# Turning x with VectorE instead of identity products on TensorE, for groups two to four of a two-layer transformer kernel

## The chip, the cores and the metric

The kernel runs on one core of one Trainium2 chip. The metric is device time in microseconds (us) for one execution. PE is TensorE, DVE is VectorE, ACT is ScalarE, POOL is GpSimd and SP is SyncE, which issues most of the DMAs. The times of the kernel before are 1934.53, 1934.77 and 1935.47 us.

## What is computed

The input x holds 32 batches of 64 tokens with 1024 features, in fp32. Two layers follow, each with a residual. What the change touches is the front of the first layer:

```python
# layer 0: a per-batch 64x64 matrix over the 64 tokens (the mixing), then a 1024x1024 weight
W = L0_cond_weights[itok_B_0_15]
mixed = einsum('bct,bcd->bdt', x, W)
x1 = x + mixed @ effective_weight.T + b_base      # effective_weight = W_base + adapters through a Fourier table
# layer 1: gate/up/down with per-batch adapters, then a product with sign(weight)
act = silu(x1 @ W_gate.T + lora) * (x1 @ W_up.T + lora)
x2 = x1 + (act @ W_down.T + lora) @ sign(L1_ffn_weight).T + bias
```

The sum x + mixed @ W needs x with features on partitions and tokens along the row, while x lies in memory with tokens as rows.

## The kernel before, in words

The 2048 tokens are worked off in four groups of 512 (`NG = 4`), counted g = 0 to 3. fp32 products are made of two words each, `hi` and `lo`: ACT writes the hi word with a copy, DVE writes the lo word with a subtraction (the helper `lo`, L918), and PE makes three products of them (L1487 to L1489). For a group: the mixing of its tokens into `mixed` (an alias of `turned`), the first layer (`first_layer`, eight output tiles `u`, whose products wait for both words of a weight tile in `split`), the seven parts of gate, up and down (`part`), the down rows, and the sign products (`sign_product`, L1698), which fill eight output tiles `o` in the eight PSUM banks in the order `OUT_BANKS = (0, 1, 2, 6, 7, 3, 4, 5)`.

Around the end of a group each engine goes through a list of its own, in program order.

- **PE**: the sign products of tiles 0 to 3 together, then tiles 4 to 7 one after another, then the mixing of the next group: eight steps `e`, each with four pairs of a mixing product (L1510, `nat_c` with `x_in`) and an identity product that turns the same tile of x (L1511). A step fills two banks (`S1_BANKS`), so three steps fit. Step 0 waits until output tile 1 has been read, step 1 for tile 5, step 2 for tile 7; step e from 3 on waits for the lo word of step e - 3. After step 6 comes half of `first_layer` tile 0, then step 7.
- **DVE**: `down_low` (lo words of the down rows, L918 hidden<-acc), then `first_weight_unit(g + 1, 0)`, the lo word of weight tile 0 (L918 split<-nat), then for each output tile `out_tile`: read with bias (L1227), add (L1231), turn (L1233); then `mixing_all`, the lo words of the eight steps, with the lo words of weight tiles 1 and 2 after steps 3 and 7; then the totals `x1_total` (L1085), which add the product, the bias and the turned x that waits in `acc`.
- **ACT**: hi words of the down rows, `move_x` for p = 0 to 3 (x_in<-nat), hi word of weight tile 0 (split<-nat), then in each mixing step a copy of the turned x into `acc` and the hi word of the mixed tile.
- **SP**: `load_x` for p = 0 to 2 behind three waits of the last part, `load_x` 3 when ACT has moved x 0 out of the slot, `load_weight` for u = 0, 1, 2 (each when ACT has moved x u + 1), then `store` of the two halves of the output, then the other weight tiles. There is one list; a wait holds everything behind it.

Of the kernel before, what the change touches and what calls it, by code (L numbers as in the profile page):

```python
# [23 lines left out]
F32 = mybir.dt.float32  # L24
# [5 lines left out]
P = 128  # L30
# [66 lines left out]
START = 1  # L97
CONSTS = 2
S1_BANKS = ((0, 2), (2, 4), (4, 6))
OUT_BANKS = (0, 1, 2, 6, 7, 3, 4, 5)  # L100

X1_BANKS = {True: (6, 7, 0, 1, 0, 1, 2, 0), False: (6, 7, 0, 1, 2, 3, 0, 1)}
# [27 lines left out]
def build_layers(nc, x, cond_index, lora_index, cond_w, W_base, b_base, enc0, enc1, coefs, masks, fourier, scratch,  # L130
# [6 lines left out]
    with ExitStack() as ctx:  # L137
        def sb(name, shape, dtype):
            return ctx.enter_context(nc.sbuf_tensor(name, shape, dtype))

        def sem(name):
            return ctx.enter_context(nc.semaphore(name))
# [67 lines left out]
        acc = sb("acc", [P, 10, G], F32)  # L210
        gated = sb("gated", [P, G], F32)
        act_f = sb("act_f", [P, G], F32)
        own_sb = sb("own_sb", [P, GB + 4], F32)
        b_col = sb("b_col", [P, KC], F32)
        bias_col = sb("bias_col", [P, KC], F32)
# [24 lines left out]
        x_moved = sem("x_moved")  # L240
        mixed_psum, mixed_hi, mixed_lo = sem("mixed_psum"), sem("mixed_hi"), sem("mixed_lo")
        xt_copied = sem("xt_copied")
        x1_psum, x1_sum, x1_hi, x1_lo = sem("x1_psum"), sem("x1_sum"), sem("x1_hi"), sem("x1_lo")
        rank_psum, rank_moved, rank_step = sem("rank_psum"), sem("rank_moved"), sem("rank_step")
        rank_words, ranks_zeroed = sem("rank_words"), sem("ranks_zeroed")
# [39 lines left out]
        def _(sp):  # L285
# [77 lines left out]
            def load_x(g, p, ahead=None):  # L363
# [5 lines left out]
                    sp.wait_ge(piece_turned, piece_number(ahead, NQ - 1, first_of(("U1", "G2", "U2")[p], g) + 2))  # L369
                sp.dma_start(nat[:, nat_slot(g, n), :], x_rows[4 * g + p]).then_inc(nat_full[nat_slot(g, n)], 128)  # L370

            def load_weight(g, u):

                n = NAT_W + u
                free_nat(g, 0, n)
                sp.wait_ge(w_stored[u], 16)
                sp.dma_start(nat[:, nat_slot(g, n), :], scratch[u]).then_inc(nat_full[nat_slot(g, n)], 128)
# [32 lines left out]
            def group(g):  # L410
                free_nat(g, 0, NAT_REM)
                for t in range(2):
                    for hq in range(4):
                        sp.dma_start(nat_quadrant(g, hq, NAT_REM)[:, 2 * t:2 * t + 2, :], rest_rows[t][hq])\
                          .then_inc(nat_full[nat_slot(g, NAT_REM)], 16)
                for k in range(2):
                    load_gate_up(g, 0, NAT_GU + k, 0, k)
                sp.wait_ge(out_stored[1], 64 * (START + g))
                load_down(0)
                load_gate_up(g, 0, NAT_GU + 2, 0, 2)  # L420
                load_part(g, 0)
                with sp.Fori(1, NQ - 1) as q:
                    load_part(g, q)
                load_sign_part(g, 6)
                for k in range(3, 6):
                    load_gate_up(g, NQ - 1, NAT_GU + k, NQ - 1, k)
                load_down_rest(g)
                load_sign_part(g, 7)
# [27 lines left out]
            for g in range(NG - 1):  # L456
                group(g)
                for p in range(3):
                    load_x(g + 1, p, g)
                load_x(g + 1, 3, g)  # L460
                for u in range(3):
                    load_weight(g + 1, u)
                store(g)
                for u in range(3, KC):
                    load_weight(g + 1, u)
# [123 lines left out]
        def rank_bank(row, word):  # L589

            return ps[row:row + 64, RANK_BANKS:RANK_BANKS + 4, P * word:P * word + P]

        def bank_of(c):
            return ps[:, T_BANK + c % 2, :]

# [8 lines left out]
        def _(act):  # L604
# [61 lines left out]

            def mixing(g, e):
                p, kh = e // 2, e % 2
                b0, b1 = S1_BANKS[e % 3]
                src = ps[:, b0:b1, :].rearrange("p a (k n t) -> p (a k) n t", k=2, n=2)  # L670
                act.wait_ge(mixed_psum, START + 8 * g + e + 1)
                copy(acc[:, 4 * kh:4 * kh + 4, P * p:P * p + P], src[:, :, 1, :]).then_inc(xt_copied, 1)
                copy(mixed[:, 0, 4 * kh:4 * kh + 4, P * p:P * p + P], src[:, :, 0, :]).then_inc(mixed_hi, 1)

            def x1_tile(g, u):
                act.wait_ge(x1_sum, 8 * g + u + 1)
# [238 lines left out]
        def _(dve):  # L915
# [157 lines left out]

            def mixing(g, e):
                p, kh = e // 2, e % 2
                b0, b1 = S1_BANKS[e % 3]
                src = ps[:, b0:b1, :].rearrange("p a (k n t) -> p (a k) n t", k=2, n=2)[:, :, 0, :]
                at = (slice(4 * kh, 4 * kh + 4), slice(P * p, P * p + P))
                dve.wait_ge(mixed_hi, 8 * g + e + 1)
                lo(mixed[:, 1, at[0], at[1]], src, mixed[:, 0, at[0], at[1]]).then_inc(mixed_lo, 1)  # L1080

            def x1_total(g, u):
                dve.wait_ge(x1_psum, 8 * g + u + 1)
                dve.wait_ge(xt_copied, 8 * g + 8)
                dve.scalar_tensor_tensor(out=acc[:, u, :], in0=ps[:, X1_BANKS[g == 0][u], :], scalar=b_col[:, u:u + 1],  # L1085
                                         in1=acc[:, u, :], op0=ALU.add, op1=ALU.add).then_inc(x1_sum, 1)

            def x1_low(g, u):
                dve.wait_ge(x1_hi, 8 * g + u + 1)
# [342 lines left out]
            def group(g, last):  # L1432
                if g > 0:
                    ranks(g)
                weight_unit(g, 0, "U0", NAT_GU + 1, SPLIT_GU + 1)
                weight_unit(g, 0, "G1", NAT_GU + 2, SPLIT_GU + 2)
                a_down_rest(g)
                act_rest(g)
                dve.wait_ge(out_stored[0], 64 * (START + g))
                part(g, 0, False, lambda g, q, i: down_first(g, i))  # L1440
                with dve.Fori(1, NQ - 1) as q:
                    part(g, q, False)
                part(g, NQ - 1, True)
                for m in range(1, KC):
                    down_low(g, m)
                if not last:
                    first_weight_unit(g + 1, 0)
                if last:
                    for o in range(8):
                        biased(o)  # L1450
                for half in range(2):
                    dve.wait_ge(out_stored[half], 64 * (START + g))
                    if half:

                        dve.wait_ge(piece_turned, piece_number(g, NQ - 1, first_of("DREM", g) + 2))
                    for o in range(4 * half, 4 * half + 4):
                        if not last:
                            out_tile(g, o, out_halves[half][:, :, 32 * (o % 4):32 * (o % 4) + 32])
                        elif o < 7:
                            last_out_tile(o)  # L1460
                        else:
                            for tokens in range(2):
                                last_out_tile(o, tokens)
                if not last:
                    mixing_all(g + 1)
                    first_layer_all(g + 1)
# [17 lines left out]
        def _(pe):  # L1484
# [9 lines left out]
            def mixing(g, e, before):  # L1494

                p, kh = e // 2, e % 2
                if kh == 0:
                    pe.wait_ge(x_moved, 4 * g + p + 1)
                    pe.wait_ge(nat_c_full[p], 32 * (g + 1))
                if e < 3:  # L1500
                    if before is not None:
                        pe.wait_ge(out_read, START + 8 * before + (2, 6, 8)[e])
                else:
                    pe.wait_ge(mixed_lo, 8 * g + e - 2)
                    pe.wait_ge(xt_copied, 8 * g + e - 2)
                for k in range(4):
                    bank = S1_BANKS[e % 3][0] + k // 2
                    dst = ps[:, bank, 256 * (k % 2):256 * (k % 2) + 256]
                    tile = x_in[:, p, P * (4 * kh + k):P * (4 * kh + k) + P]
                    pe.matmul(dst[:, 0:P], tile, nat_c[:, p, :], start=True, stop=True)  # L1510
                    mm = pe.matmul(dst[:, P:], tile, ident[:], is_transpose=True, start=True, stop=True)  # L1511
                mm.then_inc(mixed_psum, 1)

            def first_layer(g, u, half=None):
# [14 lines left out]
                for k in range(KC):  # L1529
                    if by_halves and half != 1 and k == 0:  # L1530
                        pe.wait_ge(half_lo, u + 1)
                    if by_halves and half != 1 and k == 4:
                        pe.wait_ge(plain_lo, u + 1)
                    if half == 1 and k % 4 == 0:
                        pe.wait_ge(mixed_lo, 8 * g + 7 + k // 4)
                        pe.wait_ge(xt_copied, 8 * g + 7 + k // 4)
                    mm = product(ps[:, X1_BANKS[g == 0][u], t], stationary(m, k), [mixed[:, s, k, t] for s in range(2)],
                                 k == 0, k == KC - 1)
                if half != 0:
# [324 lines left out]
```

## Time and profile before

| | us |
|---|---|
| median of three runs | 1934.77 |
| span of the profiled execution | 1933.5 |
| PE busy | 1908.3 (99%) |
| DVE busy | 1471.4 (76%) |
| ACT busy | 764.9 (40%) |
| POOL busy | 542.0 (28%) |

The span is counted from the first to the last instruction of the one profiled execution; the device time of the runs has about 1.3 us more around it. Busy is the sum of an engine's instructions without overlap; a share of 99% on PE says that it hardly ever waits, not that each of its instructions is as short as it can be. In rows of the trace the first number is the start in us, the second the time that the row covers.

### The profile page before, as it was taken

How to read it: one execution, taken by the hardware profiler on the slowest of the kernel's cores; microseconds unless marked ns; L12 is line 12 of the kernel's file. 1: busy time of each engine (PE TensorE's matmuls, PEld its weight loads, DVE VectorE, ACT ScalarE, POOL GpSimd, SP SyncE). 2: the span in 40 equal slices, each digit the busy share in tenths (PEclk: the TensorE clock that was granted, in tenths of full speed). 3: DMA queues.
4: the chain of work that ended last, by engine and by line, in shares of the span. 5: the costliest groups of instructions: out<-in, count | busy, mean ns of one | idle time of the engine just before them, and what ended most of it. 6: DMA issues, size and time to landing. Idle time of an engine off the chain costs nothing.

```text
span 1933.5 us, 31400 instructions
## 1 busy us (share of the span) xinstructions
PE 1908.3 (99%) x9080; PEld 1602.9 (83%) x9080; DVE 1471.4 (76%) x2459; ACT 764.9 (40%) x1441; POOL 542.0 (28%) x935
## 2 busy tenths in 40 slices
PE   7999999999999999999999999999999999999998
PEld 6878888888988888888898888888889888888887
DVE  6877777778678777777777877777877787777786
ACT  4443333334344333333444434333335443334331
POOL 4642222213415212211523322212071322222100
PEclk9999999999999999999999999999999999999999
DMA  9764444543566454444447655454234655555411
GB/s 232 176 124 108 104 99 109 121 94 83 136 142 130 102 116 101 103 99 84 130 110 141 127 111 116 102 116 100 69 112 127 133 122 111 120 110 115 98 44 44
DMA packets 320629, 218.38 MB, mean 113 GB/s; under 512 B 177192, under 2 KB 311208, under 8 KB 320544
## 3 DMA queue, kind: packets, MB, share of 16 engines
q1 hardware_dynamic: 281952, 188.43, 43.3%
q0 software_dynamic: 36352, 24.19, 6.7%
q10 hardware_dynamic: 2240, 4.72, 0.7%
q8 instruction: 42, 0.69, 0.2%
q14 instruction: 43, 0.35, 0.1%
HBM read 204.35 MB, written 12.58 MB: 112 GB/s over the span
## 4 chain that ended last, share of the span: by engine, by line
PE 91%; DVE 4%; ACT 2%; issue 2%; DMA 0%; SPq 0%; DVEq 0%; ACTq 0%
PE ps L1487 25%; PE ps L1489 25%; PE ps L1488 25%; PE ps L1698 6%; PE ps L1625 2%; DVE ps L932 2%; PE ps L1545 2%; PE ps L1546 2%; PE ps L1510 1%; DVE split L918 1%; PE ps L1564 1%; PE ps L1511 1%; ACT split L631 0%; DMA fourier_table<-fourier 0%; PE ps L1744 0%
## 5 line engine op out<-in xcount | busy, mean ns | idle before, releaser
L1487 PE MATMUL ps<-x,split 128*128 128x512 f32 x1376 | 538.4, 391 | 2.8 <-DVE split L918 2.5
L1489 PE MATMUL ps<-x,split 128*128 128x512 f32 x1376 | 536.4, 390 | 0.0
L1488 PE MATMUL ps<-x,split 128*128 128x512 f32 x1376 | 535.6, 389 | 0.0
L631 ACT ACTIVATE split<-ps 128x512 fp32r<-128x512 f32 x344 | 203.0, 599 | 451.4 <-DVE ps L932 442.2
L530 POOL DMA_DIRECT2D nat_ad<-L_cond_A_down x224 | 136.9, 618 | 733.1 <-DVE ps L932 723.8
L1489 PEld LDWEIGHTS ps<-x,split 128*128 128x128 f32 x1376 | 258.3, 188 | 55.8
L1488 PEld LDWEIGHTS ps<-x,split 128*128 128x128 f32 x1376 | 258.6, 188 | 54.7
L1487 PEld LDWEIGHTS ps<-x,split 128*128 128x128 f32 x1376 | 259.0, 188 | 52.5 <-DVE split L918 4.4
L1487 PE MATMUL ps<-hidden 128*128 128x512 f32 x672 | 261.6, 389 | 0.0
L1488 PE MATMUL ps<-hidden 128*128 128x512 f32 x672 | 261.6, 389 | 0.0
L1489 PE MATMUL ps<-hidden 128*128 128x512 f32 x672 | 261.5, 389 | 0.0
L918 DVE TENSOR_TENSOR split<-ps,split 128x512 fp32r<-128x512 f32 (+1 forms) x376 | 243.3, 685 | 18.0 <-ACT split L631 5.6
L932 DVE STREAM_TRANSPOSE ps<-nat 128x512 f32<-128x512 f32 x344 | 225.4, 701 | 0.6
L1170 DVE TENSOR_TENSOR acc<-ps,acc 128x512 f32<-128x512 f32 x200 | 135.1, 688 | 47.6 <-PE ps L1489 47.6
L524 POOL DMA_DIRECT2D nat_b<-L_cond_B_gate x224 | 123.9, 553 | 161.6 <-DVE ps L932 149.1
L631 ACT ACTIVATE hidden<-ps 128x512 fp32r<-128x512 f32 x184 | 109.2, 598 | 143.5 <-DVE ps L932 138.1
L1489 PEld LDWEIGHTS ps<-hidden 128*128 128x128 f32 x672 | 126.1, 188 | 26.2
L1487 PEld LDWEIGHTS ps<-hidden 128*128 128x128 f32 x672 | 126.2, 188 | 26.1
L1488 PEld LDWEIGHTS ps<-hidden 128*128 128x128 f32 x672 | 126.2, 188 | 25.9
L932 DVE STREAM_TRANSPOSE ps<-nat_down 128x512 f32<-128x512 f32 x176 | 140.9, 846 | 0.0
L1154 DVE TENSOR_TENSOR act_f<-ps,gated 128x512 f32<-128x512 f32 x84 | 57.9, 690 | 97.4 <-PE ps L1546 97.0
L606 ACT ACTIVATE hidden<-act_f 128x512 fp32r<-128x512 f32 (+1 forms) x88 | 55.6, 632 | 188.8 <-DVE act_f L1154 179.8
(141 smaller groups left out, 2745.6 us busy)
## 6 DMA issues: line engine op xcount, KB each, us to landing
nat<-L_cond_W_gate SPq DMA_DIRECT2D x336, 128.0 KB
nat<-L_cond_W_up SPq DMA_DIRECT2D x336, 128.0 KB
nat_down<-L_cond_W_down SPq DMA_DIRECT2D x112, 384.0 KB, 6.4
nat_a<-L_ffn_weight SPq DMA_DIRECT2D x128, 128.0 KB, 2.8
nat<-effective_weight SPq DMA_DIRECT2D x24, 512.0 KB
nat<-x SPq DMA_DIRECT2D x16, 512.0 KB
nat_b<-L_cond_B_gate POOLq DMA_DIRECT2D x224, 24.0 KB, 2.2
nat_b<-L_cond_B_up POOLq DMA_DIRECT2D x224, 24.0 KB, 2.2
```

The costliest lines, as they stand in the source:

```text
L524: pool.dma_start(nat_b[32 * (b // 2):32 * (b // 2) + 32, t, :, b % 2, :], b_rows[t][bass.ds(part, 1), bass.ds(i, 1)].rearrange("q a f b c ...
L530: pool.dma_start(nat_ad[b % 2::2, b // 2, :], ad_rows[bass.ds(part, 1), bass.ds(i, 1)].rearrange("q a f r c -> (q a f) r c"))\
L606: return act.activation(dst, src, ACT.Copy)
L631: act.activation(dst, src, func).then_inc(piece_hi, 1)
L918: return dve.tensor_tensor(dst, full, hi.bitcast(F32), ALU.subtract)
L932: dve.transpose(dst, src).then_inc(piece_turned, 1)
L1154: dve.tensor_tensor(act_f[:], ps[:, (2 * j + 1) % 3, :], gated[:], ALU.mult).then_inc(up_read, 1)
L1170: dve.tensor_tensor(acc[:, i, :], ps[:, DOWN_BANKS[i], :], acc[:, i, :], ALU.add).then_inc(down_added, 1)
L1487: pe.matmul(dst, a[0], b[0], start=first, stop=False)
L1488: pe.matmul(dst, a[0], b[1], start=False, stop=False)
L1489: return pe.matmul(dst, a[1], b[0], start=False, stop=last)
L1698: mm = pe.matmul(ps[:, OUT_BANKS[o], :], signs[:, m, P * o:P * o + P], down(s, m), start=(m == 0 and s == 0), stop=(m == KC - 1 and s == 1))
```

## The change

Group 0 stays as it was. For groups 1 to 3:

- SP loads x a second time, in pieces of 32 tokens by a quarter of the features (`load_x_quads`, four DMAs of 128 KB for each of four p), into two buffers: one new (`x_quads`) and one in the part of `nat_down` that the output doesn't use. p = 0 and 1 are issued before `load_x` 3, p = 1 behind a wait for the DREM pieces; p = 2 and 3 are issued after `load_x` 3 and ahead of the three weight tiles, each when DVE has turned p - 2.
- DVE turns each into `acc` with one transpose of 128x1024 (`turn_x`): p = 0 and 1 after `down_low`, p = 2 and 3 after the lo word of weight tile 0 and ahead of the output tiles.
- PE makes no identity products in these groups. A mixing step takes one bank, four steps fit (`MIX_BANKS`), and steps 0 to 3 wait for output tiles 0, 1, 2 and 5 to be read (`MIX_AFTER`); step e from 4 on waits for the lo word of step e - 4.
- ACT makes one copy in a step instead of two.

```diff
+MIX_BANKS = 4
+MIX_AFTER = (1, 2, 3, 6)
...
+        x_quads = [sb("x_quads", [P, H], F32), nat_down[:].rearrange("p a b -> p (a b)")[:, 2 * H:3 * H]]
...
+            x_quad_rows = x.rearrange("(n tq t) (hq c) -> n hq t tq c", tq=4, t=32, hq=4)
+
+            def load_x_quads(g, p):
+
+                if p == 1:
+                    sp.wait_ge(piece_turned, piece_number(g - 1, NQ - 1, first_of("DREM", g - 1) + 2))
+                elif p >= 2:
+                    sp.wait_ge(xt_turned, 4 * (g - 1) + p - 1)
+                for hq in range(4):
+                    sp.dma_start(x_quads[p % 2][32 * hq:32 * hq + 32, :].rearrange("p (b c) -> p b c", b=4),
+                                 x_quad_rows[4 * g + p, hq]).then_inc(x_quad_full[p % 2], 16)
...
                 for p in range(3):
                     load_x(g + 1, p, g)
+                for p in range(2):
+                    load_x_quads(g + 1, p)
                 load_x(g + 1, 3, g)
+                for p in range(2, 4):
+                    load_x_quads(g + 1, p)
                 for u in range(3):
                     load_weight(g + 1, u)
                 store(g)
...
@@ ACT, mixing @@
-                copy(acc[:, 4 * kh:4 * kh + 4, P * p:P * p + P], src[:, :, 1, :]).then_inc(xt_copied, 1)
-                copy(mixed[:, 0, 4 * kh:4 * kh + 4, P * p:P * p + P], src[:, :, 0, :]).then_inc(mixed_hi, 1)
+                if g == 0:
...
+                copy(mixed[:, 0, 4 * kh:4 * kh + 4, P * p:P * p + P], mix_bank(g, e)).then_inc(mixed_hi, 1)
...
@@ DVE @@
+            def turn_x(g, p):
+
+                dve.wait_ge(x_quad_full[p % 2], 128 * (g - 1) + 64 * (p // 2 + 1))
+                dve.wait_ge(down_lo, 8 * g)
+                dve.transpose(acc[:, 0:KC, P * p:P * p + P].rearrange("p k (b t) -> p k b t", b=4),
+                              x_quads[p % 2].rearrange("p (b k h) -> p k b h", b=4, k=KC)).then_inc(xt_turned, 1)
...
                 if not last:
+                    for p in range(2):
+                        turn_x(g + 1, p)
                     first_weight_unit(g + 1, 0)
+                    for p in range(2, 4):
+                        turn_x(g + 1, p)
...
@@ PE, mixing @@
+                if g > 0:
+                    if e < MIX_BANKS:
+                        pe.wait_ge(out_read, START + 8 * before + MIX_AFTER[e])
+                    else:
+                        pe.wait_ge(mixed_lo, 8 * g + e - MIX_BANKS + 1)
+                    for k in range(4):
+                        tile = x_in[:, p, P * (4 * kh + k):P * (4 * kh + k) + P]
+                        mm = pe.matmul(ps[:, e % MIX_BANKS, P * k:P * k + P], tile, nat_c[:, p, :], start=True, stop=True)
+                    mm.then_inc(mixed_psum, 1)
+                    return
```

On SP, at the end of group 0, before (names: `nat` holds x and weight tiles as loaded, `effective_weight` is the scratch in HBM, L370 is `load_x`, L377 `load_weight`, L383 `store`):

```order
L370 DMA nat<-x 128x1024 [waits piece_turned] x3
L370 DMA nat<-x 128x1024 [waits x_moved]
L377 DMA nat<-effective_weight 128x1024 [waits w_stored0,x_moved]
L377 DMA nat<-effective_weight 128x1024 [waits w_stored1,x_moved]
L377 DMA nat<-effective_weight 128x1024 [waits w_stored2,x_moved]
```

and now, where L386 is `load_x_quads` and its rows into nat_down are those of the second buffer:

```order
L375 DMA nat<-x 128x1024 [waits piece_turned] x3
L386 DMA x_quads<-x 32x4x256 x4
L386 DMA nat_down<-x 32x4x256 [waits piece_turned]
L386 DMA nat_down<-x 32x4x256 x3
L375 DMA nat<-x 128x1024 [waits x_moved]
L386 DMA x_quads<-x 32x4x256 [waits xt_turned]
L386 DMA x_quads<-x 32x4x256 x3
L386 DMA nat_down<-x 32x4x256 [waits xt_turned]
L386 DMA nat_down<-x 32x4x256 x3
L394 DMA nat<-effective_weight 128x1024 [waits w_stored0,x_moved]
```

Eight DMAs and two waits on `xt_turned`, which DVE raises, now stand between the last x tile and weight tile 0.

On DVE, at the same place, before:

```order
L918 TENSOR_TENSOR hidden<-acc,hidden 128x512 [waits down_hi] x7
L918 TENSOR_TENSOR split<-nat,split 128x1024 [waits plain_hi]
L1227 SCALAR_TENSOR_TENSOR gated<-ps,bias_col,x 128x512 [waits out_sum,out_psum,out_stored0]
L1231 TENSOR_TENSOR act_f<-gated,x 128x512 [waits out_turned,out_read]
L1233 STREAM_TRANSPOSE out_sb<-act_f 128x16x32 [waits out_sum]
```

and now:

```order
L949 TENSOR_TENSOR hidden<-acc,hidden 128x512 [waits down_hi] x7
L1125 STREAM_TRANSPOSE acc<-x_quads 128x8x128 [waits down_lo,x_quad_full0]
L1125 STREAM_TRANSPOSE acc<-nat_down 128x8x128 [waits down_lo,x_quad_full1]
L949 TENSOR_TENSOR split<-nat,split 128x1024 [waits plain_hi]
L1125 STREAM_TRANSPOSE acc<-x_quads 128x8x128 [waits down_lo,x_quad_full0]
L1125 STREAM_TRANSPOSE acc<-nat_down 128x8x128 [waits down_lo,x_quad_full1]
L1267 SCALAR_TENSOR_TENSOR gated<-ps,bias_col,x 128x512 [waits out_sum,out_psum,out_stored0]
```

Two transposes stand on either side of the lo word of weight tile 0, all of them ahead of the first output tile.

On PE no row is moved: at each of the three places the 32 identity products (L1511) are gone from between the mixing products, and the products around them stand in the order they had.

## Rows read from the trace of the kernel before

**Rows 1.** The page's first part: busy time, share of span, instructions by engine
```profile
PE 1908.3 (99%) x9080; PEld 1602.9 (83%) x9080; DVE 1471.4 (76%) x2459; ACT 764.9 (40%) x1441; POOL 542.0 (28%) x935
```

**Rows 2.** Who PE waited for: engine, line <- releaser: total us, times, longest
```profile
PE ps L1545 <- DVE lora_b_rem L918: 3.3, 1, 3.3
PE ps L1487 <- DVE split L918: 2.5, 5, 1.4
```

**Rows 3.** Timeline of PE, mixing of group 1: start, us, engine, line, operation, tiles
```profile
507.10 0.38 PE L1510 MATMUL ps<-nat_c,x_in 128*128 128x128 f32 x2
507.32 0.27 PE L1511 MATMUL ps<-ident,x_in 128*128 128x128 f32 x1
507.43 0.39 PE L1510 MATMUL ps<-nat_c,x_in 128*128 128x128 f32 x2
...
516.33 0.36 PE L1487 MATMUL ps<-turned,split 128*128 128x256 f32 x1
```

**Rows 4.** Groups by line: busy us, mean ns of one, idle time before
```profile
L932 DVE STREAM_TRANSPOSE ps<-nat_down 128x512 f32<-128x512 f32 x176 | 140.9, 846 | 0.0
...
L1511 PE MATMUL ps<-ident,x_in 128*128 128x128 f32 x128 | 34.9, 273 | 0.0
...
L1297 DVE STREAM_TRANSPOSE base_t<-base 128x1024 f32<-128x1024 f32 x8 | 9.9, 1236 | 0.0
```

**Rows 5.** Timeline of DVE from the end of group 0 into group 1
```profile
478.93 4.30 DVE L918 TENSOR_TENSOR hidden<-acc,hidden 128x512 fp32r<-128x512 f32 x7
490.09 1.23 DVE L918 TENSOR_TENSOR split<-nat,split 128x1024 fp32r<-128x1024 f32 x1 [6.86 <-ACT split L606]
491.49 0.75 DVE L1227 SCALAR_TENSOR_TENSOR gated<-ps,bias_col,x 128x512 f32<-128x512 f32 x1 [0.17 <-PE ps L1698]
...
504.16 0.71 DVE L1227 SCALAR_TENSOR_TENSOR gated<-ps,bias_col,x 128x512 f32<-128x512 f32 x1
...
507.30 0.75 DVE L1227 SCALAR_TENSOR_TENSOR gated<-ps,bias_col,x 128x512 f32<-128x512 f32 x1 [0.96 <-PE ps L1698]
...
508.81 0.71 DVE L1233 STREAM_TRANSPOSE nat_down<-act_f 128x512 f32<-128x512 f32 x1
509.75 0.69 DVE L918 TENSOR_TENSOR turned<-ps,turned 128x512 fp32r<-128x512 f32 x1 [0.22 <-ACT turned L606]
```

**Rows 6.** Timeline of ACT, the same stretch
```profile
486.87 1.06 ACT L606 ACTIVATE x_in<-nat 128x1024 f32<-128x1024 f32 x1 [2.00 <-DMA nat<-x]
489.00 1.06 ACT L606 ACTIVATE split<-nat 128x1024 fp32r<-128x1024 f32 x1 [1.07 <-DMA nat<-effective_weight]
```

**Rows 7.** Timeline of SP's queue: issues of DMAs
```profile
404.32 1.75 SPq L359 DMA_DIRECT2D nat_a<-L_ffn_weight  x4
...
450.31 2.87 SPq L359 DMA_DIRECT2D nat_a<-L_ffn_weight  x4
...
483.00 0.35 SPq L370 DMA_DIRECT2D nat<-x  x1
...
483.94 0.35 SPq L377 DMA_DIRECT2D nat<-effective_weight  x1
```

**Rows 8.** Stretches: length; busy PE, PEld, DVE, ACT, POOL; clock, DMA share, GB/s
```profile
98.00:100.00 2.00, 0.32 (x1) 0.32 (x2) 0.92 (x3) 0.97 (x4) 0.00 (x0) 0.88 0.00 0
100.00:102.00 2.00, 2.00 (x9) 1.81 (x8) 1.85 (x4) 1.11 (x2) 0.00 (x0) 0.50 0.04 11
102.00:104.00 2.00, 2.00 (x8) 1.43 (x8) 1.87 (x4) 0.85 (x2) 0.00 (x0) 0.77 0.81 227
135.00:137.00 2.00, 2.00 (x10) 1.63 (x10) 1.30 (x4) 0.63 (x1) 1.64 (x3) 1.00 1.31 199
484.00:491.50 7.50, 7.50 (x35) 6.22 (x34) 1.24 (x2) 2.99 (x3) 6.95 (x13) 1.00 0.93 289
```

**Rows 9.** Timeline of DVE at the end of group 1, first and last output tile
```profile
965.62 0.75 DVE L1227 SCALAR_TENSOR_TENSOR gated<-ps,bias_col,x 128x512 f32<-128x512 f32 x1
...
980.98 0.75 DVE L1227 SCALAR_TENSOR_TENSOR gated<-ps,bias_col,x 128x512 f32<-128x512 f32 x1 [0.52 <-PE ps L1698]
```

More of the change, by code:

```diff
@@ L242, in build_layers @@
         xt_copied = sem("xt_copied")
+        x_quad_full, xt_turned = [sem("x_quad_full0"), sem("x_quad_full1")], sem("xt_turned")
         x1_psum, x1_sum, x1_hi, x1_lo = sem("x1_psum"), sem("x1_sum"), sem("x1_hi"), sem("x1_lo")
@@ L418, in group @@
                 sp.wait_ge(out_stored[1], 64 * (START + g))
+                if g > 0:
+                    sp.wait_ge(xt_turned, 4 * g)
                 load_down(0)
@@ L591, in rank_bank, with mix_bank @@
             return ps[row:row + 64, RANK_BANKS:RANK_BANKS + 4, P * word:P * word + P]
+        def mix_bank(g, e):
+            if g > 0:
+                return ps[:, e % MIX_BANKS, :].rearrange("p (k t) -> p k t", k=4)
+            b0, b1 = S1_BANKS[e % 3]
+            return ps[:, b0:b1, :].rearrange("p a (k n t) -> p (a k) n t", k=2, n=2)[:, :, 0, :]
         def bank_of(c):
@@ L668, in mixing @@
                 p, kh = e // 2, e % 2
-                b0, b1 = S1_BANKS[e % 3]
-                src = ps[:, b0:b1, :].rearrange("p a (k n t) -> p (a k) n t", k=2, n=2)
                 act.wait_ge(mixed_psum, START + 8 * g + e + 1)
-                copy(acc[:, 4 * kh:4 * kh + 4, P * p:P * p + P], src[:, :, 1, :]).then_inc(xt_copied, 1)
-                copy(mixed[:, 0, 4 * kh:4 * kh + 4, P * p:P * p + P], src[:, :, 0, :]).then_inc(mixed_hi, 1)
+                if g == 0:
+                    b0, b1 = S1_BANKS[e % 3]
+                    src = ps[:, b0:b1, :].rearrange("p a (k n t) -> p (a k) n t", k=2, n=2)
+                    copy(acc[:, 4 * kh:4 * kh + 4, P * p:P * p + P], src[:, :, 1, :]).then_inc(xt_copied, 1)
+                copy(mixed[:, 0, 4 * kh:4 * kh + 4, P * p:P * p + P], mix_bank(g, e)).then_inc(mixed_hi, 1)
             def x1_tile(g, u):
@@ L1075, in mixing @@
                 p, kh = e // 2, e % 2
-                b0, b1 = S1_BANKS[e % 3]
-                src = ps[:, b0:b1, :].rearrange("p a (k n t) -> p (a k) n t", k=2, n=2)[:, :, 0, :]
+                src = mix_bank(g, e)
                 at = (slice(4 * kh, 4 * kh + 4), slice(P * p, P * p + P))
@@ L1083, in x1_total @@
                 dve.wait_ge(x1_psum, 8 * g + u + 1)
-                dve.wait_ge(xt_copied, 8 * g + 8)
+                if g == 0:
+                    dve.wait_ge(xt_copied, 8)
+                else:
+                    dve.wait_ge(xt_turned, 4 * g)
                 dve.scalar_tensor_tensor(out=acc[:, u, :], in0=ps[:, X1_BANKS[g == 0][u], :], scalar=b_col[:, u:u + 1],
                                          in1=acc[:, u, :], op0=ALU.add, op1=ALU.add).then_inc(x1_sum, 1)
+            def turn_x(g, p):
[3 more added lines that the diff above has]
+                              x_quads[p % 2].rearrange("p (b k h) -> p k b h", b=4, k=KC)).then_inc(xt_turned, 1)
             def x1_low(g, u):
@@ L1499, in mixing @@
                     pe.wait_ge(nat_c_full[p], 32 * (g + 1))
[L1500 to L1505, printed above, removed]
+                if g > 0:
+                    if e < MIX_BANKS:
+                        pe.wait_ge(out_read, START + 8 * before + MIX_AFTER[e])
+                    else:
+                        pe.wait_ge(mixed_lo, 8 * g + e - MIX_BANKS + 1)
[4 more added lines that the diff above has]
+                    return
+                if e >= 3:
+                    pe.wait_ge(mixed_lo, e - 2)
+                    pe.wait_ge(xt_copied, e - 2)
                 for k in range(4):
@@ L1535, in first_layer @@
                         pe.wait_ge(mixed_lo, 8 * g + 7 + k // 4)
-                        pe.wait_ge(xt_copied, 8 * g + 7 + k // 4)
+                        if g == 0:
+                            pe.wait_ge(xt_copied, 7 + k // 4)
                     mm = product(ps[:, X1_BANKS[g == 0][u], t], stationary(m, k), [mixed[:, s, k, t] for s in range(2)],
```

## The prediction

> **What bounds the kernel now.** I read the page's first part to see which engine has no room, the waits of PE to see whether it ever stands still, and then the timelines of PE, DVE, ACT and SP around one group's end, since all that the change touches lies there. PE is busy for 99% of the span [rows 1]. The waits that show are in group 0 for the most part: one of 3.3 us, and five that make 2.5 us together [rows 2]. In the mixing of groups 1 to 3 PE doesn't wait. So a product taken away there is worth its time on PE, and a wait put there costs its full length, for nothing later on PE is idle enough to give it back.
>
> I count from T, the start of the first mixing product of a group: 507.10 us for group 1 [rows 3]. DVE reads the last output tile 0.20 us later, at 507.30 [rows 5]; by the same distance T is 980.78 for group 2 [rows 9], and group 3 looks like group 2.
>
> **What is removed from PE.** A pair of mixing and identity product takes 507.43 - 507.10 = 0.33 us, and of it the identity product has 507.43 - 507.32 = 0.11 us, the mixing product 0.22 us [rows 3]. The 28 pairs up to 516.33 us give the same 0.33 each. A group drops 32, so 3.5 us, and three groups 10.6 us. The row of these products has 273 ns for one [rows 4], but that is from start to end; they overlap, and the distance of starts is what a removed one gives back.
>
> The Trainium skill ("TensorE: Matmul & The Clock Gate", Part 4: PE-mode transpose) puts a 128x128 transpose on PE at about 275 ns within a kernel. The trace agrees with it as a duration (273 ns) and not as a price (0.11 us apart); by the figure of that page of the Trainium skill the 96 would give back an estimated 26.4 us.
>
> **What is removed from ACT**: one copy in each mixing step. ACT isn't what is waited for there, so nothing.
>
> **What is added on DVE.** Four transposes of 128x1024 in a group. The kernel before has one transpose of this shape, between two tiles in SBUF, at 1236 ns; a strided source into PSUM costs 846 for half as much, so 1.69 us is the other end [rows 4]. The source here has rows of 32 words in order, like the first, so I take 1.2 us. Turns 0 and 1 fall into DVE's idle 6.86 us ahead of weight tile 0: down_low ends at 478.93 + 4.30 = 483.23, and the next work starts at 490.09 [rows 5]. They are covered by the wait for the weight. Turns 2 and 3 stand behind the weight and ahead of output tile 0, where no idle time is, so the output tiles start 2.4 us later (2.4 to 3.4).
>
> **What is moved on SP**, and this is the larger part. Before, the load of x 3 goes out at 483.00 and that of weight tile 0 at 483.94 [rows 7]; they are used at 486.87 and 489.00 [rows 6]. Now the four DMAs of x_quads 2 wait for turn 0, which ends at 483.23 + 1.24 = 484.5; four DMAs of this form take 1.75 us to issue (2.87 where much is queued) [rows 7], so they are out at 486.2. The next four, whose turn has ended by 485.7, are out at 488.0, and weight tile 0 goes at about 488.2, 4.3 us later than before. If the issue decides, it takes the 3.87 us from issue to use that x 3 had and is used at 492.1, 3.1 us late. If the DMA engines decide, the two loads ahead of it count: x 3 and the three weight tiles, 4 x 512 KB, moved at a DMA share of 0.93 and 289 GB/s [rows 8], so 1.8 us for 512 KB and 3.6 us for two; with pieces of 1 KB perhaps 2.3 each, 4.6. I take 4.0 us (3.1 to 4.6; 5.7 with the slow issue rate and a slow turn 0).
>
> Queued behind this load are the hi word on ACT, the lo word on DVE, and behind it in DVE's list turns 2 and 3, all eight output tiles and all lo words of the mixing. Weight tile 0 itself isn't needed by PE until after mixing step 6, but the output tiles are needed before.
>
> **What is late next.** Output tile 0 starts at 491.49, T - 15.6, in group 1 [rows 5] and at T - 15.2 in group 2 [rows 9]. With 4.0 + 2.4 us more it is T - 9.2 and T - 8.8. Tiles on DVE follow each other at (504.16 - 491.49) / 6 = 2.11 us, and the last takes 508.81 + 0.71 - 507.30 = 2.2 us [rows 5], so the eight take 7 x 2.11 + 2.2 = 17.0 us: DVE is done at T + 7.8 and T + 8.2. Then comes the lo word of step 0, 0.69 us [rows 5]: T + 8.5 and T + 8.9.
>
> PE makes steps 0 to 3 without a stop, in four banks, 16 x 0.22 = 3.5 us (tile 5, for step 3, is read by T - 9.2 + 5 x 2.11 + 0.75 = T + 2.1). Step 4 needs the lo word of step 0. PE stands from T + 3.5 to T + 8.5 or 8.9: 5.0, 5.35 and 5.35 us, 15.7 us in all. From then on DVE's lo words, 0.69 us each, run ahead of PE's steps of 0.88 us; the lo word of weight tile 1 is made by T + 12, before first_layer tile 1 asks for it. I find no second wait. The stores and weight tile 3 go out some 9 us after T instead of 2.5 to 6, and weight tile 3 is copied only after the first total, about T + 21.
>
> **The clock.** In group 0 PE idled 3.3 us up to 99.7 us [rows 2], and the granted clock then was 0.88, 0.50 and 0.77 in three stretches of 2 us: the 1.2 GHz level in place of 2.4 for a time worth 0.24 + 1.0 + 0.46 = 1.7 us. After the longest wait on split, 1.4 us, it stayed at 1.00 [rows 2, 8]. A stall of 5 us is on the side of the first. So 3 x 1.7 = 5.1 us.
>
> **The sum.** -10.6 + 15.7 + 5.1 = +10.2 us. On the profiled execution that makes 1933.5 + 10.2 = 1943.7 us of span; the median of the runs shown, 1934.77, stands 1.3 above the span, so 1945.0 us. The low end, a load 3.1 us late: 0.9 less in each group, +7.5. The high end: 1.7 us more by the load and 1.0 by slow turns, in three groups 8.1 more, +18.3.
>
> **The rivals.**
>
> *The saving stays.* If weight tile 0 comes no later than now (SP's eight issues and the extra megabyte fall into slack), only turns 2 and 3 delay the tiles: DVE has the lo word of step 0 at T - 15.6 + 2.4 + 17.0 + 0.7 = T + 4.5 (T + 4.9 in the others), the stalls are 1.0, 1.4 and 1.4 us, too short for the clock by the 1.4 us wait, and the sum is -10.6 + 3.8 = -6.8: 1928 us. For it: PE sheds work for certain, and DVE has 6.86 us of idle time. Against: SP's list is in order, and the DMA engines are at 0.93 just then [rows 8]. It turns at a load about 2.3 us late, stalls of 3.5 us a group with the clock kept; with the clock lost, at stalls of 1.8 us.
>
> *The clock holds.* The same stalls without the lower clock: +5.1, 1939.9 us. Only one idle stretch of that length stands in the trace, and what came before it was another mix of work.
>
> *A heavier queue.* The high ends above together, +18, some 1953 us. For it: x_quads in 1 KB pieces with POOL's small DMAs beside them; against: the transposes have the shape of the cheap row.
>
> *Identity products cost their whole duration.* With 273 ns each the saving is 26.2 us and the sum -5.4: 1929 us. The starts 0.11 us apart speak against it. The page of the Trainium skill named above would have it so.
>
> **How the numbers follow.** Forecast 0.58, clock holds 0.15, heavier queue 0.13, saving stays 0.12, full duration 0.02. A measurement of this kernel can tell about 0.2%, 3.9 us, from no change. Faster: the last two, 0.13 of their 0.14. Within 0.2%: 0.09, the low edges of the forecast and of the held clock and 0.01 of the fast side. Slower: 0.78. The range runs from 1936, below the held clock, to 1956, above the heavier queue, and leaves out the fast side and some of the tails.
>
> **What would show it.** In the changed kernel's trace: PE's busy time some 10 us lower and no identity products after group 0; SP issuing weight tile 0 about 5 us after x 3 rather than 1; ACT's copy of it some 4 us later than T - 18; DVE idle ahead of weight tile 0 shorter than 6.86 us by the two turns but longer by the delay; output tile 0 at about T - 9; on PE one wait of about 5 us before mixing step 4 in each of groups 1 to 3, released by the lo word of step 0 (turned, written by DVE), and a granted clock of 0.5 behind it. The prediction is wrong if that wait is under 3 us, if weight tile 0 is used by T - 16, or if a turn takes far from 1.2 us.

## The result and the profile after

The changed kernel takes 1948.2 us (median of five runs, 1945.31 to 1949.05) against 1935.47 us of the kernel before beside it. The ratio is 1.0063, with a 95% interval of 1.0052 to 1.0073: slower by 0.6%, 12.7 us between the medians. The forecast was 1945.0 us, and the range of 1936 to 1956 holds it.

The first part of its page, which answers to [rows 1]:

```profile
span 1946.5 us, 31238 instructions
...
PE 1904.3 (98%) x8984; PEld 1597.8 (82%) x8984; DVE 1483.9 (76%) x2471; ACT 754.4 (39%) x1417; POOL 542.1 (28%) x935
```

PE is busy for 4.0 us less, though 96 products are gone, and the span is 13.0 us longer. The waits of PE (line, releaser, us in total, times, longest) say where the time is, as [rows 2] did before:

```profile
PE ps L1551 <- DVE turned L949: 15.6, 3, 5.2
PE ps L1796 <- DMA fourier_table<-fourier: 14.7, 1, 14.7
PE ps L1597 <- DVE lora_b_rem L949: 3.3, 1, 3.3
```

L1551 is now the mixing product, and the releaser is the lo word of a mixed tile. Three waits of 5.2 us stand where there were none. The timeline of PE at the mixing of group 1:

```profile
508.48 3.78 PE L1551 MATMUL ps<-nat_c,x_in 128*128 128x128 f32 x32
517.45 4.41 PE L1551 MATMUL ps<-nat_c,x_in 128*128 128x128 f32 x24 [5.19 <-DVE turned L949]
521.62 0.36 PE L1531 MATMUL ps<-turned,split 128*128 128x256 f32 x1
```

T is 508.48. Four steps of four products (the trace has two records for each) run without a listed wait, then step 4 waits until T + 8.97. Steps 4 to 6 are twelve products, 2.6 us at 0.22 us between starts, and take 4.2. The stretches behind the stall show why (columns as in [rows 8]):

```profile
516.00:518.00 2.00, 0.55 (x2) 0.58 (x3) 1.99 (x4) 0.00 (x0) 0.00 (x0) 0.79 0.17 39
518.00:520.00 2.00, 2.00 (x11) 2.00 (x11) 2.00 (x3) 0.47 (x1) 0.00 (x0) 0.50 0.94 203
520.00:522.00 2.00, 2.00 (x17) 2.00 (x17) 1.22 (x3) 0.83 (x3) 0.00 (x0) 0.86 0.95 225
```

The granted clock is 0.50, the 1.2 GHz level, in the middle one. It is 0.79 in the first, in which PE still stands for the most part, and comes back in the course of the third; the next stretch of 2 us has 1.00. Upstream of the stall, SP's queue, ACT and DVE, to be read beside [rows 5 to 7]:

```profile
484.38 0.37 SPq L375 DMA_DIRECT2D nat<-x  x1
485.99 1.74 SPq L386 DMA_DIRECT2D x_quads<-x  x4
487.77 1.85 SPq L386 DMA_DIRECT2D nat_down<-x  x4
489.74 1.34 SPq L394 DMA_DIRECT2D nat<-effective_weight  x3
```

```profile
488.06 1.06 ACT L636 ACTIVATE x_in<-nat 128x1024 f32<-128x1024 f32 x1 [1.81 <-DMA nat<-x]
495.29 1.06 ACT L636 ACTIVATE split<-nat 128x1024 fp32r<-128x1024 f32 x1 [6.17 <-DMA nat<-effective_weight]
```

```profile
484.72 1.25 DVE L1125 STREAM_TRANSPOSE acc<-x_quads 128x1024 f32<-128x1024 f32 x1
485.89 1.20 DVE L1125 STREAM_TRANSPOSE acc<-nat_down 128x1024 f32<-128x1024 f32 x1
496.38 1.23 DVE L949 TENSOR_TENSOR split<-nat,split 128x1024 fp32r<-128x1024 f32 x1 [9.29 <-ACT split L636]
497.52 1.24 DVE L1125 STREAM_TRANSPOSE acc<-x_quads 128x1024 f32<-128x1024 f32 x1
498.68 1.20 DVE L1125 STREAM_TRANSPOSE acc<-nat_down 128x1024 f32<-128x1024 f32 x1
499.81 0.71 DVE L1267 SCALAR_TENSOR_TENSOR gated<-ps,bias_col,x 128x512 f32<-128x512 f32 x1
...
516.01 0.71 DVE L1273 STREAM_TRANSPOSE nat_down<-act_f 128x512 f32<-128x512 f32 x1
516.65 2.44 DVE L949 TENSOR_TENSOR turned<-ps,turned 128x512 fp32r<-128x512 f32 x4
```

The DMA of weight tile 0 goes out 5.4 us after that of x 3 (0.9 before), ACT waits 6.17 us for it (1.07 before), DVE waits 9.29 us for ACT (6.86 before), and then has turns 2 and 3 and eight output tiles in one unbroken row until 516.65, where the first lo word of the mixing starts. Its first result releases PE at 517.45.

### The profile page after: what moved, and what is told of

The parts are those of the page before. It is cut to its first block, busy times and chain, and to the rows that moved or that the text cites. A ratio compares the mean times of both kernels' runs of the same rounds, so it can differ in the third digit from the quotient of the medians.

```text
span 1946.5 us, 31238 instructions
## 1 busy us (share of the span) xinstructions
PE 1904.3 (98%) x8984; PEld 1597.8 (82%) x8984; DVE 1483.9 (76%) x2471; ACT 754.4 (39%) x1417; POOL 542.1 (28%) x935
## 4 chain that ended last, share of the span: by engine, by line
PE 87%; DVE 6%; issue 3%; ACT 2%; DMA 1%; SPq 1%; DVEq 0%; ACTq 0%
PE ps L1531 25%; PE ps L1533 25%; PE ps L1532 25%; PE ps L1750 4%; PE ps L1677 2%; DVE ps L963 2%; PE ps L1597 2%; PE ps L1598 2%; DVE split L949 1%; PE ps L1551 1%; DVE gated L1267 1%; DVE act_f L1271 1%; DMA base<-L_ffn_W_base 1%; PE ps L1616 1%; ACT split L661 0%
## 5 line engine op out<-in xcount | busy, mean ns | idle before, releaser
L949 DVE TENSOR_TENSOR hidden<-ps,hidden 128x512 fp32r<-128x512 f32 x184 | 126.4, 691 | 4.3
```

What stands on the lines that cost most here:

```text
L949: return dve.tensor_tensor(dst, full, hi.bitcast(F32), ALU.subtract)
```

## The experiments

All ran beside the kernel before; its medians were 1935.25 us in the first four and 1935.63 us in the other four. The theory has three parts: the load of weight tile 0 is late because eight DMAs stand ahead of it; turns 2 and 3 add their own time ahead of the output tiles; the clock falls behind the stall. The chief rivals: that one of the first two is all of it, that the loads or the DVE work cost something elsewhere, and that the clock costs nothing.

### Weight tile 0 ahead of x_quads 2 and 3

```diff
                 load_x(g + 1, 3, g)
+                load_weight(g + 1, 0)
                 for p in range(2, 4):
                     load_x_quads(g + 1, p)
-                for u in range(3):
+                for u in range(1, 3):
                     load_weight(g + 1, u)
```

> The changed kernel with one edit: SP issues the load of weight tile 0 ahead of the four DMAs of x_quads 2 and the four of x_quads 3. My theory (the tiles are late because weight tile 0 is queued behind those eight DMAs): ACT uses weight tile 0 at about T - 18 as before the change instead of T - 13; turn 3 now waits for its load (about T - 13), so output tile 0 is at about T - 11.4 instead of T - 8.7, the stall before mixing step 4 falls from 5.2 us to about 2.5 us, the time from 1948 to about 1940 us, and to 1935 if the clock no longer drops. Rival (the DVE work of the turns ahead of the tiles is what costs, wherever the loads stand): no change, 1948 us.

It took 1943.18 us, a ratio of 1.0037 (1.0024 to 1.0051) to the kernel before, 5 us better than the changed kernel. SP's queue and DVE's timeline:

```profile
485.22 0.37 SPq L394 DMA_DIRECT2D nat<-effective_weight  x1
485.89 1.75 SPq L386 DMA_DIRECT2D x_quads<-x  x4
```

```profile
492.75 1.23 DVE L950 TENSOR_TENSOR split<-nat,split 128x1024 fp32r<-128x1024 f32 x1 [5.77 <-ACT split L637]
494.26 1.25 DVE L1126 STREAM_TRANSPOSE acc<-x_quads 128x1024 f32<-128x1024 f32 x1 [0.28 <-DMA x_quads<-x]
497.02 1.25 DVE L1126 STREAM_TRANSPOSE acc<-nat_down 128x1024 f32<-128x1024 f32 x1 [1.52 <-DMA nat_down<-x]
498.19 0.71 DVE L1268 SCALAR_TENSOR_TENSOR gated<-ps,bias_col,x 128x512 f32<-128x512 f32 x1
```

T is 508.38. The load goes out at T - 23.2, where it did before the change (483.94 in [rows 7]), but ACT uses the weight at T - 16.7 and not at T - 18: from issue to use it takes 6.4 us in place of 5.1, with the eight loads of x_quads issued right behind it. Its lo word starts at T - 15.6 rather than T - 12.1, and the turns now wait for their own loads, turn 3 until T - 11.4 where I had expected T - 13. So the place in the queue had in part only been traded. Output tile 0 starts at T - 10.2 instead of T - 11.4, and the three stalls are 3.7, 4.0 and 3.3 us, 11.0 together, where I had expected 2.5 each. The rival that only DVE's work counts falls, since 5 us came back by SP's order alone; my own figure of 1940 us was too good by 3 us.

### Turns 2 and 3 behind the output tiles

```diff
                     first_weight_unit(g + 1, 0)
-                    for p in range(2, 4):
-                        turn_x(g + 1, p)
...
                 for e in range(8):
                     mixing(g, e)
+                    if e == 6:
+                        for p in range(2, 4):
+                            turn_x(g, p)
```

> The changed kernel with one edit: DVE makes turns 2 and 3 after the lo word of mixing step 6, behind the output tiles; SP's list is as changed. My theory: weight tile 0 stays late (ACT uses it at T - 13), the output tiles start 2.4 us sooner, the stall is 2.8 us instead of 5.2, so about 1941 us, 1936 if the clock then holds. Rival (turns 2 and 3 are the whole cause): the stall is gone, 1925 us. Rival (only the queue counts, DVE has slack for the turns): 1948 us.

It took 1941.97 us, a ratio of 1.0034 (1.0023 to 1.0044). PE's timeline at group 1 (T is 508.16):

```profile
515.55 5.43 PE L1552 MATMUL ps<-nat_c,x_in 128*128 128x128 f32 x24 [3.66 <-DVE turned L949]
520.67 0.43 PE L1532 MATMUL ps<-turned,split 128*128 128x256 f32 x1
```

The three stalls are 3.66, 3.09 and 3.12 us, 9.9 together in place of 15.6: 5.7 us less of stall and 6.2 us less of time, near the 7.2 that 2.4 us a group would be. The stalls were expected at 2.8 us each; in group 1 weight tile 0 is used at T - 12.5, later still than the T - 13.2 of the changed kernel. Neither rival holds: the turns are a part, and not the whole.

### Both

> Both edits together: weight tile 0 loaded ahead of x_quads 2 and 3, and turns 2 and 3 behind the output tiles. My theory: nothing stands ahead of the output tiles any more that did not before, no stall over 0.5 us, the clock holds, and the saving of 96 identity products at 0.11 us each is left: 10.6 us under the kernel before, about 1925 us. Rival (a part of the loss comes from more DMA traffic or from the four banks): 1930 to 1940 us with waits elsewhere on PE.

The two edits together, with nothing else, took 1925.86 us, a ratio of 0.9950 (0.9935 to 0.9966). No wait of PE on a mixed tile is left in groups 1 to 3. Of the 10.6 us that the removed products are worth, 9.4 are there. So the two things ahead of the output tiles are the loss; the extra 6 MB from memory, the four banks and the work on DVE cost about 1 us, too little to tell from nothing here, where they don't stand ahead of something that PE waits for. One edit alone gave 5 or 6 us of the 22. They don't add up, since each leaves the other's obstacle in place: with the weight early, the turns stand ahead of the tiles and wait for their loads; with the turns late, the weight is late. And each leaves stalls of over 3 us, behind which the clock still falls.

### All four loads early

```diff
+        x_quads = [sb("x_quads", [P, H], F32), nat_down[:].rearrange("p a b -> p (a b)")[:, 2 * H:3 * H],
+                   x_in[:, 2], x_in[:, 3]]
...
-                elif p >= 2:
-                    sp.wait_ge(xt_turned, 4 * (g - 1) + p - 1)
+                elif p == 2:
+                    sp.wait_ge(up_psum, START + TILES * g)
...
-                for p in range(2):
+                for p in (0, 2, 3, 1):
                     load_x_quads(g + 1, p)
                 load_x(g + 1, 3, g)
-                for p in range(2, 4):
-                    load_x_quads(g + 1, p)
...
+                if p >= 2 and g > 0:
+                    act.wait_ge(xt_turned, 4 * (g - 1) + p - 1)
...
-                    for p in range(2):
+                    for p in (2, 3, 0, 1):
                         turn_x(g + 1, p)
                     first_weight_unit(g + 1, 0)
-                    for p in range(2, 4):
-                        turn_x(g + 1, p)
```

> The changed kernel with all four x_quads loaded early: p = 2 and 3 go into the places of x_in that move_x 2 and 3 fill later (free once PE has used the last U2 weight), nothing of it stands between x 3 and weight tile 0, and DVE makes the four turns (2, 3, 0, 1) in its idle time ahead of weight tile 0; ACT waits with move_x 2 and 3 for turns 2 and 3. My theory: no stall, weight tile 0 used at about T - 17.5, about 1925 us (10.6 less than before). Rival (turns or loads delay something else, such as x 2 and 3 on ACT and with them weight tile 0 by 1 to 2 us): 1927 to 1932 us with a stall on PE of up to 2 us before step 4.

It took 1925.41 us, a ratio of 0.9950 (0.9936 to 0.9963), 9.8 us under the kernel before and 22 to 23 us under the changed one. DVE and PE at the end of group 0 (T is 507.68):

```profile
483.91 2.37 DVE L1126 STREAM_TRANSPOSE acc<-x_in 128x1024 f32<-128x1024 f32 x2
486.21 1.20 DVE L1126 STREAM_TRANSPOSE acc<-x_quads 128x1024 f32<-128x1024 f32 x1
487.33 1.20 DVE L1126 STREAM_TRANSPOSE acc<-nat_down 128x1024 f32<-128x1024 f32 x1
491.11 1.23 DVE L950 TENSOR_TENSOR split<-nat,split 128x1024 fp32r<-128x1024 f32 x1 [2.58 <-ACT split L635]
492.26 0.74 DVE L1268 SCALAR_TENSOR_TENSOR gated<-ps,bias_col,x 128x512 f32<-128x512 f32 x1
```

```profile
507.68 6.41 PE L1550 MATMUL ps<-nat_c,x_in 128*128 128x128 f32 x56
513.85 0.36 PE L1530 MATMUL ps<-turned,split 128*128 128x256 f32 x1
```

All four turns lie in the idle time of 6.86 us of [rows 5], of which 2.58 are left, and output tile 0 starts at T - 15.4. PE goes through seven steps in 6.17 us without a wait, where before it took 9.23 [rows 3]. This is the change with its cost removed: weight tile 0 is used at T - 17.7, and there is no stall.

### The identity products put back

```diff
                         tile = x_in[:, p, P * (4 * kh + k):P * (4 * kh + k) + P]
+                        pe.matmul(ps[:, e % MIX_BANKS, P * k:P * k + P], tile, ident[:], is_transpose=True, start=True, stop=True)
                         mm = pe.matmul(ps[:, e % MIX_BANKS, P * k:P * k + P], tile, nat_c[:, p, :], start=True, stop=True)
```

> The kernel with all four x_quads loaded and turned early, with the 96 identity products put back on PE: each is made into the place that its mixing product overwrites next, and nobody reads it. Theory (an identity product costs the 0.11 us between starts): +10.6 us against the same kernel without them, 1925.4 to 1936. Rival (it costs its whole 273 ns): +26 us, 1951.6. Rival (it is hidden beside weight loads): under +5 us.

It took 1935.89 us (1935.29 to 1936.64), 10.5 us more than without them and the same as the kernel before (1.0001, 0.9992 to 1.0011). The two ran on different chips; taken each against the kernel before beside it, the difference is 10.1 us. 10.5 / 96 is 0.109 us for each (0.106 with 10.1). The rival with 273 ns falls, and so does the one that hides them.

### The second load of x alone, in the kernel before

```diff
+                if g > 1 or p >= 2:
+                    sp.wait_ge(x_quad_full[p % 2], 128 * (g - 1) + 64 * (p // 2))
...
                 for p in range(3):
                     load_x(g + 1, p, g)
+                for p in range(2):
+                    load_x_quads(g + 1, p)
                 load_x(g + 1, 3, g)
+                for p in range(2, 4):
+                    load_x_quads(g + 1, p)
                 for u in range(3):
                     load_weight(g + 1, u)
```

> The kernel before with the second load of x alone: the four x_quads of each of groups 1 to 3 are loaded at the places of the change (2 and 3 between x 3 and weight tile 0, behind the landing of the piece before in the same buffer), and nobody reads them; the identity products and the banks are as before. Theory (the queue ahead of weight tile 0 is most of the loss): ACT uses weight tile 0 at about T - 13.5 instead of T - 18, output tile 0 starts at T - 11, PE waits before mixing steps 2 and 3, 2.8 us a group, together about +8 us, 1943 us. Rival (an extra 2 MB a group is hidden): 1935 us.

It took 1943.82 us, a ratio of 1.0041 (1.0027 to 1.0055): 8.2 us for loads that nobody reads. SP's queue, ACT's weight tile 0 and PE's waits:

```profile
484.57 1.88 SPq L383 DMA_DIRECT2D x_quads<-x  x4
488.46 1.35 SPq L391 DMA_DIRECT2D nat<-effective_weight  x3
```

```profile
494.58 1.06 ACT L626 ACTIVATE split<-nat 128x1024 fp32r<-128x1024 f32 x1 [5.70 <-DMA nat<-effective_weight]
```

```profile
PE ps L1530 <- DVE gated L1247: 4.3, 3, 1.6
...
PE ps L1530 <- DVE turned L938: 1.5, 4, 0.4
```

T is 508.26, so the weight is used at T - 13.7, 4.4 us late, and output tile 0 starts at T - 11.5. PE waits for output tile 7 to be read (before step 2, 1.4 to 1.6 us) and for the lo word (before step 3, 0.4 us). Between starts the seven steps take 11.5, 11.5 and 11.7 us in place of 9.2, so 7.0 us of the loss are there; 1.2 us more lie ahead of T in group 1. The clock stays at 1.00 in these groups, and no wait in them is longer than 1.6 us. The rival that 2 MB more are hidden falls.

These loads wait for no turn of DVE: the first of x_quads 2 goes out 0.4 us after x 3 (484.15), where in the changed kernel it is 1.6. All the same the weight is nearly as late. Its load goes out 3.4 us later than before by T, for the eight DMAs ahead of it take 3.9 us to issue, and then it takes 6.1 us from issue to use in place of 5.1.

### PE kept at work during the stall

```diff
                     else:
+                        if e == MIX_BANKS:
+                            for _ in range(20):
+                                pe.matmul(ps[:, 7, :], down(0, 1)[:, 0:P], down(1, 1), start=True, stop=True)
                         pe.wait_ge(mixed_lo, 8 * g + e - MIX_BANKS + 1)
```

> The changed kernel with 20 products of 128x512 whose result is thrown away, ahead of mixing step 4 of groups 1 to 3, where PE stands still (20 x 0.225 = 4.5 us of the 5.2). Theory (the clock's fall behind the stall costs 1.7 us a group): the idle time left is under 1 us, the granted clock stays at 1.00, and the time falls by 5.1 us against the changed kernel run beside it, 1948 to 1943. Rival (the low clock is hidden by waits for VectorE or costs less): within 1 us of the changed kernel.

> The changed kernel itself, beside the others on the same chip, so that the filled one is compared with it: 1948 us, a stall of 5.2 us before mixing step 4 of groups 1 to 3.

The changed kernel took 1947.51 us in these runs, with the filler 1942.7: 4.8 us less, with 60 products more. The filled kernel's timeline and clock:

```profile
510.60 4.83 PE L1550 MATMUL ps<-hidden 128*128 128x512 f32 x20
515.95 2.94 PE L1554 MATMUL ps<-nat_c,x_in 128*128 128x128 f32 x24 [0.52 <-DVE turned L949]
```

```profile
516.00:518.00 2.00, 2.00 (x18) 2.00 (x19) 2.00 (x4) 0.60 (x1) 0.00 (x0) 1.00 0.83 185
```

Step 4 still starts at T + 8.97 (T is 506.98), just where it did in the changed kernel, so the lo word comes no sooner and only the clock differs: 1.00, and the 24 records take 2.94 us instead of 4.41. The low clock was worth 1.6 us a group.

## Why the prediction was right, point by point

- **The saving on PE.** Forecast 3.5 us a group, 10.6 in all. Without stalls the stretch from T to the next ranks of group 1 (the first product of x with hidden) is 51.3 us, against 54.8 before: 3.5 us. Putting the products back cost 10.5 us. Starts, not durations, were the right price. The sign that PE's busy time would be some 10 us lower did not come: it is 4.0 us lower, for the most part because the low clock stretches the products behind the stalls (4.8 us by the filler); without stalls it is 9.6 lower (1898.7).
- **DVE's turns.** Forecast 1.2 us each; 1.25 and 1.20 in the trace, with 1.13 to 1.17 from one start to the next.
- **SP's list.** Forecast: tile 0's load goes out 4.3 us later than before and is used 4.0 us late. Measured from T it is used at T - 13.2, against T - 18.1 in [rows 6]: 4.9 us late in group 1, 4.6 and 4.5 in the others. This is the term that was mis-sized, and the error isn't in the issue: the first of the eight went out 1.6 us after x 3 (forecast 1.5), they took 1.74 and 1.85 us, and the weight's load went out 4.4 us later than before by T. It lies between issue and use, 5.55 us in the trace, where it had been 5.06 before and the forecast of 4.0 left 4.8. The DMA engines moved 217 GB/s over 484 to 494 us in place of the 289 of [rows 8], at a busy share of 0.90, and where the weight's load went first, and in the kernel before with the loads added, the way from issue to use was 6.4 and 6.1 us. So the list and the engines both had a part, where the forecast took one or the other to decide.
- **The output tiles and step 4.** Forecast: tile 0 at T - 9.2 and T - 8.8, step 4 at T + 8.5 and 8.9. Measured: T - 8.7, - 8.2 and - 8.4, and T + 9.0, 9.4 and 9.3. The forecast stalls of 15.7 us were 15.6 by the row of waits, but that agreement is in part luck: counted between starts, as the forecast counts, they are 17.1. The 1.4 us come from the later output tiles, and a small part is a second wait that the forecast didn't find, 0.2 us before step 3 of group 2 for output tile 5 to be read.
- **The clock.** Forecast 1.7 us a group from a single stretch of group 0. Measured by the filler: 1.6. That the two are so near is luck as well: a part of the 0.24 in the forecast's sum fell while PE still stood, and the loss behind a stall was anything from 1.4 to 2.5 us in these kernels (below). The prediction's list of waits also leaves out the longest, 13.8 us for the Fourier table ahead of PE's first product. It is in both kernels and no term of the sum, but the sentence that only one idle stretch of that length stands in the trace is wrong; behind this one the granted clock reads 1.00, which no run here explains.
- **The sum.** From T to the same point behind the first layer, the groups are 3.5, 4.0 and 4.0 us longer, 11.5 us, against the forecast 10.2. The rest of the 13.0 us of span, 1.4 us, lies ahead of the first mixing of group 1 (T is 508.48 instead of 507.10), in the part that the change doesn't touch; 0.9 us of it is the wait for the Fourier table (14.7 us instead of 13.8), which was anything from 13.5 to 14.7 us in the profiles of all these kernels. The changed kernel run again began that mixing at 507.66, so much of the 1.4 us is scatter from one execution to the next. The forecast of the median also took 1.3 us around the span; the profiled execution has 1.7 (1948.2 and 1946.5).
- **The rivals.** "The saving stays" needed a weight that comes no later; it came 4.5 to 4.9 us late. Even with the weight's load issued in time the kernel took 1943.2 us and not 1928, since the turns then wait for their own loads; the saving came only with the turns out of the way of the tiles too. "The clock holds" is refuted by the rows of 0.50 and by the filler. "A heavier queue" (1953 us) is 5 us off, the forecast 3: the turns were cheap, the weight late by more than 4.0 us and less than 5.7. "Full duration" falls with the products put back, 10.5 us and not 26.

## What to carry to other kernels

When an engine that never waits is relieved, what pays for it has to be looked for in the lists that stand ahead of its next wait, and there what counts is the place in the list and not the amount of work: with the same loads and the same four turns the kernel was 12.7 us slower than before at one place and 9.8 us faster at another. A load that is needed soon should not stand behind loads that are needed later, on a queue that issues in order; here their mere issue, 3.7 us for eight, made up most of the delay, and their wait for a turn of DVE about 1 us. And a product on a pipelined engine is worth the distance of starts, here 0.11 us, not the duration in the trace, 0.27.

## What the runs showed of the hardware that was not expected

A shorter stall can cost more clock than a longer one, as far as one profile of each kernel shows. In the kernel with the late turns, the stall of 3.66 us in group 1 was followed by these stretches:

```profile
514.00:516.00 2.00, 0.45 (x2) 0.48 (x3) 1.97 (x5) 0.00 (x0) 0.00 (x0) 0.50 0.12 28
516.00:518.00 2.00, 2.00 (x11) 2.00 (x11) 2.00 (x4) 0.36 (x1) 0.00 (x0) 0.50 0.94 205
518.00:520.00 2.00, 2.00 (x12) 2.00 (x11) 0.99 (x3) 0.83 (x2) 0.00 (x0) 0.50 0.96 227
520.00:522.00 2.00, 2.00 (x15) 2.00 (x15) 1.02 (x2) 0.60 (x1) 0.00 (x0) 0.80 0.91 240
```

PE was back at 515.55 and the low clock lasted into the last of them, 2.5 us lost (5.43 us for the 24 records in place of 2.94); a stall of 3.09 us in the next group lost 1.6, and the 5.19 us of the changed kernel 1.5. With the weight's load first, 3.72, 3.96 and 3.32 us lost 2.5, 1.4 and 2.5: 6.5 us in all, against 4.8 in the changed kernel. So a part of what that edit gained in stalls went to the clock. What sets the length of the low stretch was not tried. At the other end, waits of 1.6 us in the kernel before with the loads left the clock at 1.00; no wait between 1.6 and 3.1 us stands in the mixing of groups 1 to 3 of any kernel here, so nothing is shown of those.
